# Row maxima of two attention heads by products on separate halves of the array's rows, with the null key's scores by short products of their own

## The reference

```python
queries = x[bidx, q_idx]                       # the 512 best rows of 1024
key_values = x[bidx, kv_idx]                   # the 256 best rows
q = jnp.einsum('bgnd,ged->bgne', queries, w_q)
kv = jnp.einsum('bgnd,ged->bgne', key_values, w_kv)
...                                            # 8 heads of 64
k = jnp.concatenate([nk, k], axis=-2)          # a null key and value in front
v = jnp.concatenate([nv, v], axis=-2)
attn = jax.nn.softmax(jnp.einsum('bghid,bghjd->bghij', q, k) * DH ** (-0.5), axis=-1)
o = jnp.einsum('bghij,bghjd->bghid', attn, v)
```

## Time and profile before

| | |
|---|---|
| time, median of 3 runs | 3632.01 us (3627.47 to 3639.0) |
| the profiled execution's own time | 3642.05 us |
| its span, first to last instruction | 3640.7 us |
| PE, PEld busy | 92%, 53% |
| DVE, ACT, POOL busy | 81%, 62%, 51% |
| mean granted clock of TensorE | 0.968 |

### The profile page before, as it was taken

One profiled execution on the slowest core, in us unless ns is written; L12 is line 12 of the kernel. 1 busy time (PEld: TensorE's weight loads), 2 busy tenths in 40 slices (PEclk: granted clock), 3 DMA queues, 4 the chain that ended last, 5 costly groups with the idle time before them and its releaser, 6 DMA issues.

```text
span 3640.7 us, 64398 instructions
## 1 busy us (share of the span) xinstructions
PE 3360.3 (92%) x24312; PEld 1940.5 (53%) x24312; DVE 2962.7 (81%) x5336; ACT 2273.6 (62%) x4329; POOL 1850.6 (51%) x1483
## 2 busy tenths in 40 slices
PE   6899999999999999999748999999999999999997
PEld 4455555555555555555424555555555555555554
DVE  6798989999898988989967777787787877787774
ACT  5767767677767666776426555566555755555564
POOL 1332433334343332323437888877665765666565
PEclk9899999999999999999868999999999999999998
DMA  5444544465554445444387576777676676577664
GB/s 160 94 109 112 114 94 102 102 128 114 116 120 81 102 114 116 116 103 84 77 127 158 101 131 119 127 147 151 120 141 128 146 133 125 115 133 136 126 113 68
DMA packets 834213, 428.02 MB, mean 118 GB/s; under 512 B 575239, under 2 KB 758663, under 8 KB 831856
## 3 DMA queue, kind: packets, MB, share of 16 engines
q1 hardware_dynamic: 777584, 320.97, 42.5%
q0 software_dynamic: 56320, 102.94, 15.9%
HBM read 176.19 MB, written 101.71 MB: 76 GB/s over the span
## 4 chain that ended last, share of the span: by engine, by line
PE 58%; DVE 14%; DMA 8%; issue 5%; POOL 5%; ACT 4%; SPq 1%; another core or an unknown queue 0%; POOLq 0%; ACTq 0%; DVEq 0%
PE pair L1314 7%; PE pair L1275 7%; PE pair L1197 7%; PE pair L1421 7%; PE pair L1245 6%; PE pair L1285 4%; PE pair L1329 3%; DMA oT<-ohl 2%; PE pair L1343 2%; PE pair L1389 2%; PE pair L1390 2%; PE pair L1359 2%; PE pair L1256 2%; PE pair L1265 2%; DMA de<-cum 2%
## 5 line engine op out<-in xcount | busy, mean ns | idle before, releaser
L2238 POOL TENSOR_TENSOR ph<-pf,ph 128x512 f16<-128x512 f32 x256 | 354.8, 1386 | 243.8 <-ACT ph L2106 241.6
L1571 DVE SCALAR_TENSOR_TENSOR cv<-raw,taps,cv 128x512 f32<-128x512 f32 x480 | 428.6, 919 | 29.1 <-ACT cv L1978 27.9
L1826 DVE TENSOR_REDUCE smx<-pair 128x2 f32<-128x514 f32 x512 | 349.7, 684 | 88.3 <-PE pair L1359 85.5
L1197 PE MATMUL pair<-xhT,whi 128*128 128x512 f16 x1280 | 385.5, 383 | 8.1 <-ACT btok L1998 2.1
L2100 ACT ACTIVATE pf<-pair 128x1024 f32<-128x1024 f32 x256 | 261.6, 1023 | 155.0 <-PE pair L1390 131.8
L1275 PE MATMUL pair<-ohi,yT 128*128 128x512 f16 x1024 | 319.8, 384 | 27.1 <-DMA yT<-yhl 25.8
L1245 PE MATMUL pair<-zhi,xhT 128*128 128x512 f16 x1024 | 326.2, 380 | 1.5 <-ACT btok L1998 1.2
L1861 DVE TENSOR_TENSOR ph<-pf,ph 128x512 f16<-128x512 f32 x256 | 254.8, 995 | 84.3 <-ACT ph L2106 81.3
L2008 ACT ACTIVATE de<-de,cum 128x128 f32<-128x128 f32 x1024 | 309.5, 388 | 1.2
L2106 ACT CAST ph<-pf 128x1024 f16<-128x1024 f32 x256 | 267.3, 1044 | 4.9 <-PE pair L1410 0.2
L1285 PEld LDWEIGHTS pair<-xdt,de 128*128 128x128 f32 x2048 | 244.7, 196 | 20.4 <-issue 12.5
(11 more groups left out here) (260 smaller groups left out, 9811.6 us busy)
## 6 DMA issues: line engine op xcount, KB each, us to landing
de<-cum SPq DMA_DIRECT2D x64, 1024.0 KB, 9.4
rows<-rowt SPq DMA_DIRECT2D x16, 1040.0 KB, 6.2
xin<-x SPq DMA_DIRECT2D x16, 1024.0 KB, 8.8
y<-xin SPq DMA_DIRECT2D x16, 1024.0 KB, 5.7
y<-ob POOLq DMA_DIRECT2D x64, 256.0 KB, 4.6
qb<-qa SPq DMA_DIRECT2D x32, 512.0 KB
rbc<-rank SPq DMA_DIRECT2D x63, 256.0 KB
wst<-wkv SPq DMA_DIRECT2D x32, 256.0 KB
```

The lines of the kernel that those rows point to most:

```text
L1197: ins = pe.matmul(bk[:], w[:, k, ws], xt[:, ha, k, :], start=n == 0, stop=n == 3 * KD - 1)
L1571: ve.scalar_tensor_tensor(c_[:], r_[:, t:t + BLK], taps[:, ct, t:t + 1], c_[:], ALU.mult, ALU.add).then_inc(done, 1)
L1826: ve.tensor_reduce(smx[:, qt, 2 * h2:2 * h2 + 2], sc[:, :, 0:NK + 1], AX.X, ALU.max)
L2238: po.tensor_tensor(p_[:, 1, 1], f[:, 1], p_[:, 0, 1], ALU.subtract).then_inc(S.plp, 1)
```

## The change

A maximum needs no low part. After the change the row maxima are taken from the high part of the queries alone: for an even head from partitions 0 to 63, for an odd head from 64 to 127. To this end the odd heads are stored the other way round, high part in 64 to 127 and low part in 0 to 63, which the score products do not notice, since `ka` has the same keys in both halves. A step `max` now issues four products: for each of the two heads one of 2 columns over all 128 rows (the null key's score, still in full precision, put behind the 257 columns in the bank), then for each head one of 257 columns over 64 rows, one in the upper and one in the lower half of the array's rows. The reductions read the same number of elements. The two ScalarE and the two VectorE instructions of a query step write other partitions, the DMA to `qb` becomes two of half the size, and the scores wait for both. In the planner's table a `max` takes 0.19 instead of 0.23, and from this its order changes in many places.

```diff
--- before.py
+++ after.py
@@ -636,7 +636,7 @@
 
     seats = {"q": "q_low", "k": "k_low", "v": "v_low", "max": "max_out", "shift_turn": "shift_out",
              "null_turn": "null_out", "score": "soft", "value": "norm_o", "out": "res"}
-    takes = {"q": 2.6, "k": 2.62, "v": 2.6, "max": 0.23, "shift_turn": 0.24, "null_turn": 0.24,
+    takes = {"q": 2.6, "k": 2.62, "v": 2.6, "max": 0.19, "shift_turn": 0.24, "null_turn": 0.24,
              "score": 0.88, "value": 0.95, "out": 2.6}
     for step in line:
         name, n, k = (*step, 0)[:3]
@@ -1356,7 +1356,10 @@
                 bk = bank("max", n, k)
                 for a in range(2):
                     h = 2 * h2 + a
-                    ins = pe.matmul(bk[:, a * 512:a * 512 + KW], qa[u][:, h, qs_], ka[u][:, h, :], start=True, stop=True)
+                    pe.matmul(bk[:, a * 512 + KW:a * 512 + KW + 2], qa[u][:, h, qs_], ka[u][:, h, NK:KW], start=True, stop=True)
+                for a in range(2):
+                    h, half = 2 * h2 + a, slice(a * DH, (a + 1) * DH)
+                    ins = pe.matmul(bk[:, a * 512:a * 512 + NK + 1], qa[u][half, h, qs_], ka[u][half, h, 0:NK + 1], start=True, stop=True)
                 ins.then_inc(S.mx_mm, 1)
 
             def shift_turn(n):
@@ -1378,7 +1381,7 @@
             def score(n, h):
                 u = n % 2
                 q.wait_ge(S.klo, KT * (n + 1))
-                q.wait_ge(S.qdup, 16 * (n + 1))
+                q.wait_ge(S.qdup, 32 * (n + 1))
                 q.wait_ge(S.shift_in, 16 * (n + 1))
                 q.wait_ge(S.pool_set, 2)
                 q.wait_ge(S.kb_id, min(n, 1) + 1)
@@ -1784,10 +1787,9 @@
             def low_queries(n, e):
                 qa_, bk = qa[n % 2], bank("q", n, e)
                 q.wait_ge(S.qa, KD * n + e + 1)
-                for a in range(2):
-                    ins = ve.scalar_tensor_tensor(qa_[DH:P, 2 * e + a, :], bk[a * DH:(a + 1) * DH, :], 1.0 / WS,
-                                                  qa_[0:DH, 2 * e + a, :], ALU.mult, ALU.subtract)
-                ins.then_inc(S.qlo, 1)
+                ve.scalar_tensor_tensor(qa_[DH:P, 2 * e, :], bk[0:DH, :], 1.0 / WS, qa_[0:DH, 2 * e, :], ALU.mult, ALU.subtract)
+                ve.scalar_tensor_tensor(qa_[0:DH, 2 * e + 1, :], bk[DH:P, :], 1.0 / WS, qa_[DH:P, 2 * e + 1, :],
+                                        ALU.mult, ALU.subtract).then_inc(S.qlo, 1)
 
             def low_keys(n, e2):
                 ka_, kb_, bk = ka[n % 2], kb[n % 2], bank("k", n, e2)
@@ -1824,7 +1826,7 @@
                 sc = bank("max", n, k)[:].rearrange("p (a t) -> p a t", a=2)
                 q.wait_ge(S.mx_mm, NP * n + k + 1)
                 ve.tensor_reduce(smx[:, qt, 2 * h2:2 * h2 + 2], sc[:, :, 0:NK + 1], AX.X, ALU.max)
-                ve.tensor_reduce(snl[:, qt, 2 * h2:2 * h2 + 2], sc[:, :, NK:KW], AX.X, ALU.add).then_inc(S.mx, 1)
+                ve.tensor_reduce(snl[:, qt, 2 * h2:2 * h2 + 2], sc[:, :, KW:KW + 2], AX.X, ALU.add).then_inc(S.mx, 1)
 
             def shift(n):
                 q.wait_ge(S.mx, NP * (n + 1))
@@ -2068,7 +2070,7 @@
                 q.wait_ge(S.q_mm, KD * n + e + 1)
                 q.wait_ge(S.s_mm, H * (n - 1))
                 ac.mul(qa_[0:DH, 2 * e, :], bk[0:DH, :], 1.0 / WS)
-                ac.mul(qa_[0:DH, 2 * e + 1, :], bk[DH:P, :], 1.0 / WS).then_inc(S.qa, 1)
+                ac.mul(qa_[DH:P, 2 * e + 1, :], bk[DH:P, :], 1.0 / WS).then_inc(S.qa, 1)
 
             def ks(n, e2):
                 ka_, bk = ka[n % 2], bank("k", n, e2)
@@ -2380,7 +2382,8 @@
                 u = n % 2
                 q.wait_ge(S.qa, KD * (n + 1))
                 q.wait_ge(S.s_mm, H * (n - 1))
-                sp.dma_start(qb[u][0:DH], qa[u][0:DH]).then_inc(S.qdup, 16)
+                sp.dma_start(qb[u][0:DH, 0:H:2], qa[u][0:DH, 0:H:2]).then_inc(S.qdup, 16)
+                sp.dma_start(qb[u][0:DH, 1:H:2], qa[u][DH:P, 1:H:2]).then_inc(S.qdup, 16)
 
             def shift_turn(n):
                 u = n % 2
```

## The result

The changed kernel takes 3663.76 us (median of 4 runs, 3659.22 to 3676.47) against 3632.32 us before (also 4 runs, 3627.47 to 3639.00; the table ahead had three of them): 1.0091 times as long, 95% interval 1.0061 to 1.0121. It is slower by 31 us, and the forecast of 3624 was wrong in its sign; the first rival had said 3668. The profiled execution took 3659.22 us, the shortest of the four.

What follows compares the result with a forecast made beforehand. TensorE was taken as the attention's bound, though not alone. Its 23 us saving, a third arriving, gave 3642.05 - 8 = 3634 us profiled, other terms 0, and a median of 3624 us; range 3608 to 3678.

Steps and rivals of the forecast that it cites:

- the first rival: Maximum step: TensorE runs empty at each height change, 363 ns a step, 72 us for 512, half arrives: 3668 us; chance 33%.
- The bound, how much arrives: Attention: TensorE bounds, not alone; at most 68% of its saving reaches the end, a third of 23 us taken: 8 us.
- the 97 us of the earlier trace: Before line 1359's products or loads: TensorE taken to stand idle some 118 times, 97 us in all, mostly awaiting VectorE.
- Up to a quarter of the steps: Of 512 maximum steps, the share before which time saved on TensorE would only be waited for.
- the third rival: Maxima: TensorE gains as worked out but VectorE takes the whole and nothing arrives: 3632 us; chance 10%.
- The short products: Maximum step: two products of 2 columns cost 26 ns each, 52 together, their weight loads hidden.
- The halves: Maximum step: two half-height products run side by side, 112 ns plus half a weight delay, 126 ns; bounds 112 to 140.
- The change between full and half height: Maximum step: running empty between heights costs 0 to 185 ns a step; 0 taken, from the 64-column weights.
- The sum for TensorE: Maximum step: 178 ns against 223, 45 ns less a step, 23 us less for 512.
- The rest of the edit: Query steps, reductions and the split copy to `qb`: 0, with 0.5 us more SP issue an item covered by slack.
- The order: Planner's moved steps across the kernel: 0 on the mean, 10 us to each side.
- The range: Whole kernel's time: 3608 to 3678 us, its upper end being the engine running empty plus 10 us for the planner's moves.

## Why the prediction was wrong

**The bound, how much arrives.** Right in the main. TensorE is the bound, with slack: I took a third for a gain and a half for a loss. Measured by the ratios: 51 to 56% of 60 to 66 us for the changed products in the old order, 36% of 95 for the change of height alone (about half without the clock), 49% of 26 for the short products (this last hardly outside its noise). One reading was wrong: the 97 us of the earlier trace rows are not TensorE's idle time. They add up what the matmuls and the weight loads waited, often the same wait twice; the matmuls alone have 36 us in about 40 places. "Up to a quarter of the steps" and the third rival's comparison with VectorE's 85.5 us rested on the larger figure.

**The short products.** Right for one of them: 26 ns taken, 28 to 39 from the first to the second. The second costs nothing of its own, since it falls into the 96 ns ahead of the first half.

**The halves.** Right in kind: they run side by side, the second 3 ns behind the first where 14 was taken. The 0.03 us between products of 65 columns, from which the 14 came, are the time of their columns (0.112 us for 258 makes 0.028) and not a delay by their weights.

**The change between full and half height.** Here it failed. The bounds were 0 and 185 ns, both from rows of the trace, and I took 0 by the row "nearest in kind", weights of 64 columns. Measured: 96 ns in and about 105 out; without the second short product's 26, which the 96 contain, 175 a step, near the upper end. The nearer relative was the weights of 8 columns with their 95 and 90 ns. The sum for TensorE was therefore not -45 but +116 to +129 ns a step, +60 to +66 us and not -23. The Trainium skill (TensorEngine Tiling, Key Properties) states that a change of tiling mode drains the engine; here the measurement agrees with it, and with the first rival, which said 363 ns a step, 72 us and 3668 (measured 0.34 to 0.35, 60 to 66 and 3664). What held against the rule, four products next to weights of 64 columns, showed that not every narrower shape is such a change; it did not show that half height is none. (The trace has that change in two places only, both with f32 products, and no run here tests it with f16.)

**The rest of the edit.** Right as to 0: query steps, reductions and the second copy cost nothing that shows. The two issues take 0.76 us more an item and not 0.5, under cover.

**The order.** The 10 us to each side were too narrow: about 14 us for this one, with an interval from nothing to 27, and 27 to 33 us (0.8 to 0.9%) between two orders of the steps of four heads.

**The range** held the time, since the rival had been kept in it with 33%. That the rival's 3668 lies so near is in part luck: its step was 11 to 22 ns too long, and it left out the order, which may have added some 14 us here.

## What to carry to other kernels

Halves of the array are worth using where many half-height products stand together: each visit costs about 200 ns in and out together, so two products of 257 columns (about 110 ns saved) do not pay for it. Four would be 20 ns ahead by an estimate from the four-head step (96 + 330 ns against 446), and there the short products took that away again. Where the profile shows two answers for a cost, the forecast should not rest on the resemblance of shapes: weigh the two by what the engine has to do differently, and take neither for granted. Where a planner orders the steps, compare in the same order, or try several, before a change of under 1% is judged, since the order alone moves the time by as much.

## What the runs showed of the hardware

Two 64-row products on different halves of the rows, into different banks, start 3 ns apart and last as one; on the same half the second starts 120 ns later instead of the 109 of full-height products with 257 columns. A switch of height costs about 96 ns more than the columns of the product ahead on the way in, and 95 to 105 on the way out, for a product of 2 columns as for one of 257. Between half-height products that follow each other, also over two maximum steps in a row, next to nothing is lost (116 to 120 ns where full height has 109). Fewer rows as such cost nothing: the products over 72 rows (line 1390 before) are 218 ns from the next, as those of 512 columns over 128 rows are 215, and the one over 96 rows is 0.03 us from the next. The change that costs is the one to 64 rows.
